# Attention units on one core: weighing the values ahead of making the scores on TensorE

## What is computed

```
q = split_heads(x @ Wq.T)
k, v       = split_heads(text @ Wk.T),    split_heads(text @ Wv.T)
k_ip, v_ip = split_heads(ip @ Wk_ip.T),   split_heads(ip @ Wv_ip.T)
out = merge_heads(softmax(q k^T / sqrt(32)) v) + merge_heads(softmax(q k_ip^T / sqrt(32)) v_ip)
return out @ Wo.T + bo + x
```

## Time and profile before

| | |
|---|---|
| time, median of 3 runs | 525.41 us (524.24 to 530.5) |
| the profiled execution | 527.97 us, its span 525.9 us |
| PE busy | 495.8 us, 94% of the span |
| DVE busy | 420.3 us, 80% |
| ACT busy | 370.0 us, 70% |
| POOL busy | 311.6 us, 59% |
| DMA | 149.15 MB, mean 284 GB/s |
| granted TensorE clock | 0.983 of full speed |

### The profile page before, as it was taken

One profiled execution on the slowest core, in us unless ns is written; L12 is line 12 of the kernel. 1 busy time (PEld: TensorE's weight loads), 2 busy tenths in 40 slices (PEclk: granted clock), 3 DMA queues, 4 the chain that ended last, 5 costly groups with the idle time before them and its releaser, 6 DMA issues.

```text
span 525.9 us, 16128 instructions
## 1 busy us (share of the span) xinstructions
PE 495.8 (94%) x5314; PEld 420.6 (80%) x5314; DVE 420.3 (80%) x650; ACT 370.0 (70%) x1691; POOL 311.6 (59%) x320
## 2 busy tenths in 40 slices
PE   7969799699999999999999999999999999999777
PEld 7958697578888888888888888888788788788565
DVE  0056733999999999999999999999999998899812
ACT  0336745778878787887888878888787888787610
POOL 2022782467676676766767666667675766755610
PEclk9969979999999999999999999999999999999999
DMA  8993731999999999999999999999999999998992
GB/s 284 409 413 140 238 110 59 299 299 302 286 289 311 298 299 314 298 308 309 301 322 295 310 308 298 312 297 298 313 290 307 307 290 302 295 301 285 300 271 78
DMA packets 104574, 149.15 MB, mean 284 GB/s; under 512 B 11744, under 2 KB 91104, under 8 KB 104416
## 3 DMA queue, kind: packets, MB, share of 16 engines
q1 hardware_dynamic: 104544, 148.77, 93.7%
HBM read 85.81 MB, written 62.91 MB: 283 GB/s over the span
## 4 chain that ended last, share of the span: by engine, by line
POOL 38%; issue 35%; PE 10%; DMA 6%; ACT 4%; SPq 3%; DVE 2%; POOLq 1%; DVEq 0%; ACTq 0%
POOL probs L362 20%; POOL res L368 9%; POOL x_lo L353 9%; DMA wq_raw<-wq_in 3%; DMA y_out<-res 3%; PE pv_ps L806 2%; PE q_ps L679 2%; PE v_ps L806 2%; ACT probs L419 1%; SPq L255 1%; POOLq L105 1%; SPq L254 1%; PE s_ps L755 1%; PE pv_ps L716 1%; PE x_ps L679 1%
## 5 line engine op out<-in xcount | busy, mean ns | idle before, releaser
L362 POOL TENSOR_TENSOR probs<-probs,row_inv 128x616 f32<-128x616 f32 x160 | 193.5, 1230 | 154.6 <-DVE row_inv L607 154.6
L419 ACT ACTIVATE probs<-s_ps,row_neg 128x77 f32<-128x77 f32 x640 | 200.5, 340 | 74.1 <-DVE row_neg L575 74.1
L419 ACT ACTIVATION_READ_ACCUMULATOR probs<-s_ps,row_neg 128x1 f32 x640 | 141.4, 221 | 0.0
L575 DVE TENSOR_REDUCE row_neg<-s_ps 128x8 f32<-128x616 f32 x160 | 120.1, 792 | 25.6 <-PE s_ps L704 22.6
L595 DVE STREAM_TRANSPOSE turned<-probs 128x512 f32<-128x512 f32 (+1 forms) x160 | 125.0, 818 | 4.5 <-POOL probs L362 4.5
L679 PEld LDWEIGHTS q_ps<-x_hi,wq_hi 128*128 128x128 f32 x400 | 58.4, 189 | 34.4 <-issue 30.0
L679 PE MATMUL q_ps<-x_hi,wq_hi 128*128 128x256 f32 x400 | 82.1, 302 | 4.1 <-DVE wq_lo L566 4.1
L602 DVE TENSOR_REDUCE row_sum<-probs 128x8 f32<-128x616 f32 x80 | 63.5, 794 | 16.4 <-ACT probs L428 16.4
L704 PE MATMUL s_ps<-keys,q 32*128 32x154 f32 x1280 | 65.1, 317 | 9.6 <-ACT q L409 4.4
L679 PE MATMUL q_ps<-x_hi,wq_lo 128*128 128x256 f32 x400 | 73.5, 281 | 0.0
L679 PE MATMUL q_ps<-x_lo,wq_hi 128*128 128x256 f32 x400 | 73.4, 281 | 0.0
(11 more groups left out here) (71 smaller groups left out, 621.7 us busy)
## 6 DMA issues: line engine op xcount, KB each, us to landing
bounce_d<-turned SPq DMA_DIRECT2D x80, 640.0 KB, 5.7
p_main<-bounce_d SPq DMA_DIRECT2D x320, 128.0 KB
res<-x_in SPq DMA_DIRECT2D x75, 128.0 KB, 5.0
y_out<-res SPq DMA_DIRECT2D x75, 128.0 KB, 4.7
x_raw<-x_in SPq DMA_DIRECT2D x70, 128.0 KB, 4.8
p_last<-bounce_d SPq DMA_DIRECT2D x80, 104.0 KB
stage<-wk_in SPq DMA_DIRECT2D x6, 640.0 KB, 8.4
stage<-wv_in SPq DMA_DIRECT2D x6, 640.0 KB, 10.7
```

What stands on the lines that cost most here:

```text
L362: nc.gpsimd.tensor_tensor(rows[:, :, keys], rows[:, :, keys], row_inv[:, u.slot, :, br].unsqueeze(2) .broadcast_to([P, GROUP * SUB, size]) ...
L419: done = nc.scalar.activation(rows[:, cols], s_ps[:, j, cols], ACT.Exp, bias=row_neg[:, j, i:i + 1], accum_out=row_sum[:, j, i:i + 1])
L575: nc.vector.tensor_reduce(row_neg[:, heads_of(half)], by_row(s_ps[:, heads_of(half), 0:SUB * BLK]), AXIS.X, ALU.max, negate=True).then_inc ...
```

## The change

In TensorE's `emit(u)` the two calls `scores(u)` and `weigh_values(u-5)` change places. The waits go with the calls. No matmul is added or removed, and the instructions of the other four engines are the same, in the same order.

```diff
             def emit(u):
 
                 chunk = u.plus(-OUT_LAG)
-                scores(u)
                 if u.plus(-VALUE_LAG).exists():
                     weigh_values(u.plus(-VALUE_LAG))
+                scores(u)
                 if u.plus(Q_AHEAD).exists():
                     project_q(u.plus(Q_AHEAD))
                 if chunk.exists():
```

## The result

| | before | changed |
|---|---|---|
| median, this comparison | 524.83 us (523.07 to 537.05, 6 runs) | 578.54 us (576.05 to 580.72, 6 runs) |
| ratio, 95% interval | | 1.1029 [1.0989, 1.1068] |
| the profiled execution | 527.97 us, span 525.9 | 577.93 us, span 575.4 |
| granted TensorE clock | 0.983 | 0.982 |

The changed kernel is 10% slower; 574 us had been predicted, with 563 to 588.

A forecast was written before the change was run, and what follows sets the result against it. TensorE, at 5.41 us a unit, was taken to bound the middle. +43.7 (longer units), +4.1 (fifth units), +1.0 (start) and -1.5 (end) gave +47.3 us, hence 575.3 or 572.7; 574 us was said, range 563 to 588.

The forecast's parts named there:

- The 5.00 us of VectorE: From the start of `scores` to the end of VectorE's `attn_lo`: 5.00 us in every unit, unable to come sooner.
- not slower: Rival: VectorE's 5.00 us shrinks by 0.6, deciding at 4.41 us after `scores`; 526 us, within 2%; chance 0.06.
- What is over 5.41: Units took 5.48 us against TensorE's 5.41; the excess is mostly 19 waits for probabilities from DRAM, 8.9 us in all.
- The start after `attn_lo`, 0.08: Time PE takes to start `weigh_values` after `attn_lo` ends: 0.08 us, between two cases of 0.05 and 0.15.
- `weigh_values` to `scores`, 1.00: On PE, from `weigh_values` to the `scores` now behind it: 1.00 us, with 0.90 to 1.10 possible.
- Every fifth unit, 6.37: Units whose `project_out` starts a tile also wait there for `attn_lo`: 6.37 us, 0.29 over the others, 14 times, +4.1 us.
- 73 units: From `scores` of unit 6 to unit 79: 6.08 us each, 443.8 against 400.1 us, +43.7.
- Start and end: `scores(6)` comes later behind `weigh_values(1)`, +1.0 us; after the last `scores`, probabilities land sooner, -1.5 us (0 to -3).
- The wait for `p_loaded` at nothing: `weigh_values` comes nearer to its `scores`, but longer units give the probabilities' loads time back: costed at nothing.
- the ring: Cycle of `scores`, maxima, subtraction, two transposes, `attn_lo`, `weigh_values`, next `scores`; its length sets the period, 6.08 us (5.95 to 6.25).
- the loads become the ring: Rival: probabilities take 31.5 us to come back instead of 29.2, period 6.5, about 605 us; chance 0.05.
- The clock: Rival: PE's 0.6 us pauses lower TensorE's granted clock to 0.50, a unit takes 9.4 us, 814 us; chance 0.03.

The follow-up runs named there:

- Experiment 2: Changed kernel, one bank, with VectorE taking `attn_low` before the two transposes instead of after them: 532.75 us, ratio to the kernel before 1.0104.
- experiment 7: Kernel before, in its old order, with SyncE fetching the residual rows one unit later: 523.24 us, ratio to the kernel before 0.9994.
- experiment 5: Changed kernel with the two waits of `weigh_values` exchanged, `attn_lo_done` first and `p_loaded` second: 576.43 us, ratio to the kernel before 1.0971.
- experiments 7 and 8: The second of these: changed kernel with `attn_low` ahead of the transposes and the residual fetched one unit later: 525.62 us, ratio to the kernel before 1.0049.
- experiment 6: Kernel before with `weigh_values` moved behind `project_q`, and ScalarE's `attn_high` one step later: 536.23 us, ratio to the kernel before 1.0232.

## Why the prediction was right

By its own steps, each against the trace after:

- **The 5.00 us of VectorE.** 5.00 and 5.01 in the two units shown. VectorE got 0.75 us of idle time before the maxima, and its chain grew no shorter for it. The rival *not slower* fell with it. Experiment 2 brought `attn_lo` under the 4.41 us at which that rival would decide, and the unit then ran on as the rival had said it would, up to the next wait.
- **What is over 5.41.** 73 x 5.41 is 394.9 us, so 5.2 of the 400.1 us were over it, put down mostly to the 8.9 us of waits for the probabilities. Without such waits the stretch still took 397.0 us (experiment 7): about 3 of the 5.2 were waits. The sum used the measured 400.1, so this reading changed nothing.
- **The start after `attn_lo`, 0.08.** It has two values, 0.05 and 0.15, and the length of the pause, by which 0.08 was chosen, does not decide between them (experiment 5): 24 units at 6.05 and 33 at 6.15 instead of 57 at 6.08. 33 x 0.07 - 24 x 0.03 = +1.6 us over the sum.
- **`weigh_values` to `scores`, 1.00,** a pair that no row had shown: 300.97 - 299.97 = 1.00.
- **Every fifth unit, 6.37.** 331.55 - 325.19 = 6.36 in the changed kernel, the start of that unit being this row of its timeline:

```profile
325.19 0.81 PE L704 MATMUL s_ps<-keys,q 32*128 32x154 f32 x16
```

- **The ends of the loop's rounds were left out.** Five of the fifth units end a round; the one that ends at 300.97 is one of them, and there `weigh_values` starts 0.60 instead of 0.31 us after the matmul at 299.37 that waits for `attn_lo`. These are its row and the `scores` before it:

```profile
294.31 0.81 PE L704 MATMUL s_ps<-keys,q 32*128 32x154 f32 x16
...
299.37 0.38 PE L679 MATMUL x_ps<-attn_lo,wo_hi 128*128 128x256 f32 x1 [0.64 <-DVE attn_lo L611]
```

  That unit took 300.97 - 294.31 = 6.66, 0.29 more; the five took 0.25 to 0.29 more, +1.3 in sum. The mean of 5.48 contained such ends, the new sum, built from steps, did not.
- **73 units.** From the two terms above, and from 0.8 in units 6 and 7 (mostly the clock, below), the stretch from `scores` of unit 6 to that of unit 79 became 541.62 - 90.04 = 451.6 us instead of the 447.9 of the sum:

```profile
90.04 0.81 PE L704 MATMUL s_ps<-keys,q 32*128 32x154 f32 x16
...
541.62 0.81 PE L704 MATMUL s_ps<-keys,q 32*128 32x154 f32 x16
```

- **Start and end.** `scores(6)` came 90.04 - 89.70 = 0.3 later, not 1.0: `weigh_values(1)` stands ahead of it with its 1.00, but what goes before ran 0.7 sooner in this execution, for which no cause was sought. The end took 575.4 - 541.62 = 33.8 instead of 36.1, -2.3 where -1.5 was said, within its bounds. Sum over all: 3.7 - 0.7 - 0.8 = 2.2 us above the predicted +47.3, and +49.5 is what the span grew by. That it is so near is in part luck, since misses of both signs cancel.
- **The wait for `p_loaded` at nothing, covered by the ring.** No such wait in the changed kernel. Experiment 2 took the cover away and the waits were there, 9.5 us on the matmuls and 13.7 on the weight loads. The cover was named rightly; the cause of these waits, full DMA engines, was not (experiments 7 and 8). It changed no number, which is luck, and it was used against the rival *the loads become the ring*. In the changed kernel SyncE's wait for a store ahead of the residual is gone as well, so with the longer unit the cause that experiment 7 found is not there either. In experiment 2, with units of 5.61 us on average, SyncE's wait was back, and where TensorE waited the loads set the period.
- **The clock.** Pauses of 0.5 to 0.7 us in every unit left it at 1.00 between 357 and 450 us, which is 2.4 GHz. The Trainium skill, "TensorE: Matmul & The Clock Gate", section "A second HAM failure mode: psum-queue depth-cycling", has short pauses between groups of matmuls make the clock of another kernel swing; the trace does not agree for pauses of this size, with 83.99 of 93 us busy.

The terms and their sizes came from one view, the timeline of a unit, with the waits as a check; the shares of busy time, 94% for PE and 80% for DVE, would have said that VectorE has room. It has: it is idle for a quarter of the span now, and TensorE waits for it in every unit.

## What to carry to other kernels

Before two steps of an engine are exchanged, write down for every wait that moves how early its value is now: here 1.15 us, against 1.74 us by which the wait came forward. If a wait that comes due too soon hangs on the work that is queued behind it, the distance is lost in every unit and not once; then either a second buffer or an earlier release on the other engine gives it back, and the next wait behind must be looked for at once. Count the changes of the array's tile shape in both orders. And where loads come late, look for a wait that blocks their queue before you blame full DMA engines.

## What was not expected of the hardware

- **The place of a wait is worth 0.1 us.** The same wait on the same value let TensorE start 0.05 or 0.13 to 0.15 us after it, by whether the weight load itself carries it. The order in which two waits are written changes that, but in the loop it only changed which units were the slow ones (experiment 5).
- **Two groups of 128 x 128 tiles, split by another shape, cost 0.20 to 0.26 us more a unit** (experiment 6); one change of shape more is the likely reason.
- **Of two equal pauses one lowered the clock.** Ahead of `weigh_values(2)` TensorE waited 2.45 us; from 95.2 to 99.0 us it was then granted 0.63 on average, between its levels of 1.2 and 2.4 GHz, and the matmuls of `scores(7)` took 1.41 us as in the earlier trace rows; by 102 us it had 1.00 again. Before the last unit it waited 2.42 us, and `scores(79)` behind that ran in 0.81, at full clock. The timeline of PE in the changed kernel:

```profile
95.26 0.64 PE L716 MATMUL pv_ps<-p_main,v 128*32 128x256 f32 x8 [2.45 <-DVE attn_lo L611]
...
96.27 1.41 PE L704 MATMUL s_ps<-keys,q 32*128 32x154 f32 x16
...
540.62 0.64 PE L716 MATMUL pv_ps<-p_main,v 128*32 128x256 f32 x8 [2.42 <-DVE attn_lo L611]
```

  So the length of the pause alone does not decide. Nor does its place: in the run of experiment 5 the pause before the last unit, 2.34 us, was followed by a granted clock of 0.50, or 1.2 GHz, from 537.8 to 541.0 us. What does decide wasn't tried. The kernel before has no pause ahead of `weigh_values(2)`, and the slow stretch there cost about 0.6 us in unit 7.
